# A conditioned residual on one core: loads moved to ScalarE's queue in 1 MB pieces, zeros and placing shared out anew

## The reference

```python
# x: (64, 64, 512) f32, itok: (64,) int32, weights: (200, 64, 64) f32
w = weights[itok]
out = x + jnp.einsum('bct,bcd->bdt', x, w)
```

## Time and profile before

| | |
|---|---|
| median of 3 runs | 47.75 us (47.55 to 47.91) |
| the profiled execution's own time | 47.52 us |
| its span | 45.6 us |
| PE, VectorE, ScalarE, GpSimd busy | 23.4, 14.9, 14.6, 2.6 us |
| moved by DMA | 17.83 MB: 9.44 read from HBM, 8.39 written |
| granted TensorE clock, mean | 0.981 of full |

### The profile page before, as it was taken

The page is one execution under the profiler, slowest core; times in us unless marked ns, Lnnn a source line. Parts: engine busy times, 40 slices in busy tenths (PEclk is TensorE's granted clock), DMA queues, the critical chain, the costliest instruction groups (busy, mean ns, idle before and its releaser), DMA issues.

```text
span 45.6 us, 301 instructions
## 1 busy us (share of the span) xinstructions
PE 23.4 (51%) x98; PEld 10.0 (22%) x98; DVE 14.9 (33%) x20; ACT 14.6 (32%) x18; POOL 2.6 (6%) x10
## 2 busy tenths in 40 slices
PE   0004000000000009999999789999999999930000
PEld 0004000000000004243527054534534434300000
DVE  0891000000003980009559290064064065550000
ACT  0820000000000009009999999062062063450000
POOL 4080900000000000000000000000000000000000
PEclk9999999999999999999999999999999999999975
DMA  0689999999999999999997999999998999999991
GB/s 0 108 338 431 424 417 431 417 439 424 431 431 511 431 403 417 388 460 460 460 331 280 403 424 453 381 489 446 460 417 338 431 446 403 424 439 388 417 406 47
DMA packets 2162, 17.83 MB, mean 391 GB/s; under 512 B 242, under 2 KB 242, under 8 KB 498
## 3 DMA queue, kind: packets, MB, share of 16 engines
q1 hardware_dynamic: 2016, 16.78, 89.1%
q0 software_dynamic: 144, 1.05, 5.4%
q10 hardware_dynamic: 2, 0.00, 0.0%
HBM read 9.44 MB, written 8.39 MB: 391 GB/s over the span
## 4 chain that ended last, share of the span: by engine, by line
PE 43%; DMA 21%; DVE 10%; ACT 7%; issue 5%; POOL 2%; POOLq 1%
PE product L156 31%; DMA gathered<-weights,table_row 21%; PE product L160 12%; DVE w_all L186 5%; ACT y_sb L116 4%; ACT w_diag L111 3%; POOL w_diag L128 2%; DVE w_diag L168 2%; DVE y_sb L195 2%; DVE gathered L183 1%; POOLq L36 1%; DVE piece L171 0%; DVE one L169 0%
## 5 line engine op out<-in xcount | busy, mean ns | idle before, releaser
L160 PE MATMUL product<-x_sb,w_all 64*64 64x512 f32 x64 | 8.9, 698 | 13.0 <-DVE w_all L186 12.9
L156 PE MATMUL product<-x_sb,w_diag 128*128 128x512 f32 x32 | 14.0, 594 | 0.3 <-issue 0.3
L191 DVE COPY y_sb<-product 128x1024 f32<-128x1024 f32 x7 | 8.6, 1225 | 12.6 <-PE product L156 7.2
L116 ACT COPY y_sb<-product 128x1024 f32<-128x1024 f32 x7 | 7.1, 1012 | 8.5 <-PE product L156 6.3
L111 ACT COPY w_diag<-w_all 64x256 f32<-64x256 f32 x8 | 5.1, 637 | 14.6 <-DVE w_all L186 14.4
L156 PEld LDWEIGHTS product<-x_sb,w_diag 128*128 128x128 f32 x32 | 6.0, 190 | 8.3 <-issue 8.3
L160 PEld LDWEIGHTS product<-x_sb,w_all 64*64 64x64 f32 x64 | 3.5, 207 | 17.6 <-DVE w_all L186 13.0
L183 DVE TENSOR_TENSOR gathered<-gathered,piece 128x64 f32<-128x64 f32 x1 | 0.3, 270 | 10.0 <-DMA gathered<-weights,table_row 10.0
L139 PE MATMUL product<-one,row_along 1*128 1x1 f32 x2 | 0.6, 344 | 3.6 <-DVE row_along L175 3.6
L186 DVE STREAM_TRANSPOSE w_all<-gathered 128x2048 f32<-128x2048 f32 x1 | 2.3, 2311 | 0.0
L195 DVE COPY y_sb<-product 128x512 f32<-128x512 f32 x2 | 1.4, 692 | 1.5 <-PE product L156 1.5
(11 more groups left out here) (4 smaller groups left out, 0.4 us busy)
## 6 DMA issues: line engine op xcount, KB each, us to landing
out<-y_sb SPq DMA_DIRECT2D x5, 1024.0 KB, 6.2
x_sb<-x SPq DMA_DIRECT2D x4, 1024.0 KB, 8.3
x_sb<-x SPq DMA_DIRECT2D x2, 2048.0 KB, 19.9
out<-y_sb SPq DMA_DIRECT2D x1, 2048.0 KB, 6.7
out<-y_sb SPq DMA_DIRECT2D x2, 512.0 KB, 4.3
condition<-conditions ACTq DMA_DIRECT2D x1, 0.2 KB
gathered<-weights,table_row POOLq DMA_INDIRECT x1, 9.7
```

Of the source, the lines that this page charges most:

```text
L116: nc.scalar.copy(y_sb[:, 4 * turn:4 * turn + 2, :], product[turn % SETS][0][:, :, :]).then_inc(moved_by_act, 1)
L156: product_of = nc.tensor.matmul(product[turn % SETS][j][:, g, :], w_diag[:, n - 4 * TILED, :], x_sb[:, n, :], start=True, stop=True)
L160: product_of = nc.tensor.matmul(product[turn % SETS][h][halves(g), j, :], w_all[halves(h), :, n], x_sb[halves(h), n, :], start=True, stop= ...
L191: nc.vector.tensor_copy(y_sb[:, 4 * turn + 2:4 * turn + 4, :], product[turn % SETS][1][:, :, :]).then_inc(moved_by_dve, 1)
```

## The change

- All loads are issued from ScalarE's queue, as eight loads of one turn each. The conditions' load and the stores are issued from the sync queue; stores too are of one turn each, and the last turn in two rounds as before. Every run is 8 KB (4 KB in the two last stores).
- The memsets of `w_diag` on VectorE (L168) and GpSimd (L128) go. VectorE sets a 128x1 tile `zero`, and ScalarE copies it, as a broadcast, over the off-diagonal blocks, two copies of 64x1024, after it has issued the loads.
- Placing is shared: ScalarE copies the upper half (`halves(0)`) and VectorE the lower (`halves(1)`), one copy of 64x256 each per turn in turns 0 to 3.
- The semaphores for zeroing and placing go, since the copies to `y_sb` behind them on the same engines already make TensorE wait. VectorE waits for `pieces_set` before the diagonal add; GpSimd no longer does.

```diff
-    LOADS = [(0, 0), (1, 1), (2, 2), (3, 3), (4, 5), (6, 7)]
-    STORES = [(0, 0), (1, 1), (2, 3), (4, 4), (5, 5), (6, 6)]
...
         @block.sync
         def _(sp):
-            for first, last in LOADS:
-                pairs = pairs_of(first, last)
-                sp.dma_start(x_sb[:, pairs, :], x[:, pairs, :]).then_inc(x_loaded[first], 16)
-            for first, last in STORES:
-                sp.wait_ge(moved_by_act, last + 1)
-                sp.wait_ge(moved_by_dve, last + 1)
-                pairs = pairs_of(first, last)
-                sp.dma_start(out[:, pairs, :], y_sb[:, pairs, :]).then_inc(stored, 16)
+            sp.dma_start(condition[:, :, :], conditions).then_inc(condition_loaded, 16)
+            for turn in range(LAST):
+                sp.wait_ge(moved_by_act, turn + 1)
+                sp.wait_ge(moved_by_dve, turn + 1)
+                sp.dma_start(out[:, pairs_of(turn), :], y_sb[:, pairs_of(turn), :]).then_inc(stored, 16)
...
         @block.scalar
         def _(act):
-            act.dma_start(condition[:, :, :], conditions).then_inc(condition_loaded, 16)
+            for turn in range(TURNS):
+                act.dma_start(x_sb[:, pairs_of(turn), :], x[:, pairs_of(turn), :]).then_inc(x_loaded[turn], 16)
+            act.wait_ge(zero_set, 1)
+            for h in range(PAIR):
+                nc.scalar.copy(w_diag[halves(h), :, (1 - h) * D:(2 - h) * D],
+                               zero[halves(h), :].unsqueeze(2).to_broadcast([C, PAIRS - 4 * TILED, D]))
+            act.wait_ge(w_ready, 1)
             for turn in range(TURNS):
                 if turn < TILED:
-                    later = slice(4 * turn, 4 * turn + 4)
-                    act.wait_ge(w_ready, 1)
-                    for h in range(PAIR):
-                        nc.scalar.copy(w_diag[halves(h), later, h * D:(h + 1) * D],
-                                       w_all[halves(h), :, pairs_of(TILED + turn, TILED + turn)].rearrange("p d n -> p n d")
-                                       ).then_inc(w_placed, 1)
+                    nc.scalar.copy(w_diag[halves(0), pairs_of(turn), 0:D],
+                                   w_all[halves(0), :, pairs_of(TILED + turn)].rearrange("p d n -> p n d"))
...
         @block.gpsimd
-            pool.wait_ge(pieces_set, 2 * (P // Q))
-            nc.gpsimd.memset(w_diag[halves(1), :, 0:D], 0.0).then_inc(w_zeroed, 1)
...
         @block.tensor
-                if turn in x_loaded:
-                    pe.wait_ge(x_loaded[turn], 16)
+                pe.wait_ge(x_loaded[turn], 16)
...
-                if turn == TILED:
-                    pe.wait_ge(w_zeroed, 2)
-                if turn >= TILED:
-                    pe.wait_ge(w_placed, PAIR * (turn - TILED + 1))
...
         @block.vector
-            nc.vector.memset(w_diag[halves(0), :, D:PAIR * D], 0.0).then_inc(w_zeroed, 1)
+            nc.vector.memset(zero[:, :], 0.0).then_inc(zero_set, 1)
...
+            dve.wait_ge(pieces_set, 2 * (P // Q))
...
+            dve.wait_ge(w_ready, 1)
             for turn in range(LAST):
+                if turn < TILED:
+                    nc.vector.tensor_copy(w_diag[halves(1), pairs_of(turn), D:PAIR * D],
+                                          w_all[halves(1), :, pairs_of(TILED + turn)].rearrange("p d n -> p n d"))
                 dve.wait_ge(multiplied, turn + 1)
```

More of the change, by code:

```diff
@@ L48, in conditioned_residual_kernel @@
         one = sbuf("one", [1, 1], fp32)
+        zero = sbuf("zero", [P, 1], fp32)
         piece = sbuf("piece", [P, K], fp32)
@@ L58, in conditioned_residual_kernel @@
                    for s in range(SETS)]
-        x_loaded = {first: semaphore(f"x_loaded{first}") for first, _ in LOADS}
+        x_loaded = [semaphore(f"x_loaded{turn}") for turn in range(TURNS)]
         condition_loaded = semaphore("condition_loaded")
         one_set = semaphore("one_set")
+        zero_set = semaphore("zero_set")
         rows_along = semaphore("rows_along")
@@ L69, in conditioned_residual_kernel @@
         w_ready = semaphore("w_ready")
-        w_zeroed = semaphore("w_zeroed")
-        w_placed = semaphore("w_placed")
         multiplied = semaphore("multiplied")
@@ L79, in halves, with pairs_of @@
             return slice(h * C, (h + 1) * C)
-        def pairs_of(first, last):
-            return slice(4 * first, 4 * last + 4)
+        def pairs_of(turn):
+            return slice(4 * turn, 4 * turn + 4)
         def round_of(turn, j):
@@ L100, in _ @@
                 sp.dma_start(out[:, round_of(LAST, j), :], y_sb[:, round_of(LAST, j), :]).then_inc(stored, 16)
-            sp.wait_ge(stored, 16 * (len(STORES) + 2))
+            sp.wait_ge(stored, 16 * (TURNS + 1))
         @block.scalar
         def _(act):
-            act.dma_start(condition[:, :, :], conditions).then_inc(condition_loaded, 16)
+            for turn in range(TURNS):
[5 more added lines that the diff above has]
+            act.wait_ge(w_ready, 1)
             for turn in range(TURNS):
                 if turn < TILED:
-                    later = slice(4 * turn, 4 * turn + 4)
-                    act.wait_ge(w_ready, 1)
-                    for h in range(PAIR):
-                        nc.scalar.copy(w_diag[halves(h), later, h * D:(h + 1) * D],
-                                       w_all[halves(h), :, pairs_of(TILED + turn, TILED + turn)].rearrange("p d n -> p n d")
-                                       ).then_inc(w_placed, 1)
+                    nc.scalar.copy(w_diag[halves(0), pairs_of(turn), 0:D],
+                                   w_all[halves(0), :, pairs_of(TILED + turn)].rearrange("p d n -> p n d"))
                 if turn < LAST:
```

## The result

| | before | after |
|---|---|---|
| median of six runs of each | 47.88 us | 48.39 us |
| profiled execution, its span | 47.52, 45.6 us | 48.08, 46.2 us |
| last copy to y_sb ends | 41.0 us | 40.0 us |

The ratio is 1.012, with a 95% interval of 1.008 to 1.017. I had forecast 47.2 us, and 48.39 is outside my range too.

The account below looks back on a forecast made before the run. Transfers were taken to bound the kernel: 0.27 (switch) plus 0.21 (8 KB runs) is 0.48 us, so the profiled 47.52 becomes 47.04. With medians 0.23 above the profiled run it expected 47.25, rounded to 47.2 us; range 46.6 to 48.1.

Parts of the forecast that it names:

- The transfers set the end: Whole kernel: DMA transfers bound it, so 1.7 us of earlier compute is worth nothing by itself.
- The front: Start, before the turns: without the memsets L175 ends 1.1 us sooner; gather issued at 3.5 rather than 4.61.
- The turns: Turns 0 to 4: shared placing stops TensorE waiting for ScalarE, 0.6 us gained; TensorE ends at 38.6.
- 8 KB instead of the 16 KB store: Stores in 30 to 35 us: 8 KB runs lift the rate from 408 GB/s, gaining 0.21 us.
- The switch: 23 to 26 us, loads to stores in one queue: two queues take back a net loss of 0.27 us.
- The mixture: From 20.6 us: loads and stores alternate on the engines for some 6.8 us at 426 GB/s.
- Rival 2: Mixed stretch: engines lose time turning from load to store packets, 366 GB/s, 1.1 us cost, 48.4 us; chance 0.16.
- Rival 1: The switch: loss comes from changing HBM reads to writes, not queue order; no telling change, 47.6 us; chance 0.25.

Follow-up runs that it names:

- e4: Kernel before with only the changed kernel's compute (ScalarE's zeros, shared placing), old load and store lists, old queues; ratio 1.006.
- e3: Kernel before with 8 KB runs alone: eight loads and seven stores of one turn, all on the sync queue; ratio 1.003 (0.999 to 1.008).
- g4: Changed kernel stripped to loads and stores, no computation; each turn stored from x_sb once its load has landed; 45.54 us.
- e1: Changed kernel with its queues undone: loads and stores from the sync queue, conditions from ScalarE's; 8 KB runs and new compute stay; ratio 1.013.
- c1: g4 with the first two turns copied inside SBUF (x_sb to y_sb) as each lands, stores after the seventh load; no time given.
- c2: g4 with the two early transfers going from HBM to HBM, other stores after the seventh load; no time given.
- e2: Kernel before with queues swapped alone: six loads with old lists from ScalarE's queue, conditions and stores from the sync queue; ratio 1.006.
- c3: g4 with the first and fifth turns stored as each lands, the rest after the seventh load; no time given.
- g3: Changed kernel with the first store held until the last load has landed; ratio 1.029 (1.020 to 1.039).
- g1: Changed kernel with the first store held until the load of turn 6 has landed; ratio 0.988, 47.41 us; second time 0.995, 47.44 us.
- g2: e1 with the first store held until the load of turn 6 has landed; ratio 0.996, 47.52 us.

## Why the prediction was wrong, point by point

- **The transfers set the end:** right, and shown by e4 and by the changed kernel itself, whose last copies ended 1.5 and 1.1 us sooner than before's, and which ran no faster for it. It holds only while the transfers are as slow as in the kernel before: in e3, without a dip, the queue was all but empty at the end, and the last copy at 41.5 came too late for a gain.
- **The front:** right. 1.1 us forecast, 1.16 measured, L165 at 0.28 us. That the memset on GpSimd had caused the 1.06 isn't shown by itself, since VectorE's memset went as well. The Trainium skill, "SBUF — State Buffer", section "Who interferes with whom", says that a two-port VectorE operation and a GpSimd one shut each other out for a whole instruction; the 1.06 us with a memset beside it and the 0.28 without agree.
- **The turns:** prices right (VectorE's placing 0.39 against 0.35, zero copies 1.04 each against 1.0); TensorE's end 39.25, within the 38 to 39.3 that I named. I had 38.6, as turns 0 to 3 took 9.25 us rather than 8.7.
- **8 KB instead of the 16 KB store: a misreading, and the second term that failed.** 429 against 408 GB/s in 30 to 35 would be 0.25 us where I had 0.21, but that is luck. The 442 of 26 to 30 and the 408 of 30 to 35 are one effect of how 16 KB packets are booked, and I used one half for each term. Together, before and after:

```profile
26.00:35.00 9.00, 8.68 (x21) 3.92 (x22) 3.68 (x3) 4.54 (x6) 0.00 (x0) 1.00 1.00 423
```

```profile
26.00:35.00 9.00, 9.00 (x22) 3.99 (x21) 3.03 (x3) 2.39 (x3) 0.00 (x0) 1.00 1.01 428
```

That is 0.1 us. e4 keeps the 16 KB store and has 437 in 30 to 35, and e3, with 8 KB runs alone, gains no time. All that the kernel before lacked in 13 to 35 us was 0.31 us, so 0.48 was not there to be gained.
- **The switch: this step failed.** I put the net loss of before at 0.27 us, took it for the order in the queue, and had it vanish with two queues. It grew instead, to 93 x 3 = 0.28 MB or 0.65 us in 23 to 26, with nothing given back behind (0.67 us over 13 to 35, where before lost 0.31). The error is in its cause. I read the rate of 23 to 26 as the place where loads end and stores begin. It is what the first long store does to loads still under way, before its own packets move, and how much of it falls on loads depends on how soon the store comes. All the microseconds gained in compute went into making that sooner. I had priced this gain at nothing; it had a negative price.
- **The mixture:** I had stores alternating with loads from 20.6 us, 6.8 us long. In the changed kernel it hardly exists, since the store's packets wait from 21.15 to 25, when the loads are nearly done. Where it does exist, in g4, it has the 426 GB/s that I took. The delay stood in the trace of before: the gather is issued at 4.61 and its packets share the engines in 9 to 10 us; the first of them move behind 8.5. I used these rows for the sharing and didn't carry over the delay.
- **Rival 2** gave 48.4 us, which is the measured time by luck, since its mechanism is wrong: an engine that loses time at each turn from load to store would have shown in g4 at 12 us, and doesn't. Rival 1 was right about the queues: one queue and two differ little, as the changed kernel and e1 show (1.012 and 1.013), and the two with the store held (0.988 and 0.995 in two trials of two queues, 0.996 with one). The Trainium skill, "DMA: Bandwidth & Descriptors", section "Issuing engines are not separate DMA queues", says that more issuing engines save issue time alone; these ratios agree. The other half of rival 1, a cost of turning to writes of HBM, falls by c1, which has the fall without any such write, and c2, which writes and has none.
- **Left over:** 0.12 us of the loss lies in 2.5 to 13 us, where the first packets are slow in every profile; whether the queues have a part in it isn't shown. Nor is why the swap alone (e2) costs 0.6%, with a dip smaller than before's; its profile has 416 GB/s over 13 to 35 us to before's 420, and the loss lies in 30 to 35 (395), not in the dip. And the bytes left at 44.5 explain 0.4 of the 0.56 us between the profiled executions; the rest is open.

## What to carry to other kernels

Where transfers bound a kernel, find the stretches in which the engines are busy and the bytes are few, and ask which transfer had just been issued; it may not have moved a byte yet. An engine that delivers sooner is not free there: look at what its results set off, and try to hold that back by one wait (here one `wait_ge` ahead of the first store, for the last but one load, turned 1.012 into 0.988 to 0.995). Hold it only so far that its start-up is still covered: held for one load more, the kernel ran at 1.029. And look at what sets the end once the transfers are faster, since e3 lost its dip and gained nothing.

## What the hardware showed that I had not expected

- The first long DMA that reads SBUF, issued while loads from HBM keep the 16 engines full, slows these loads to 284 to 298 GB/s over 3 us (7 to 10 us in g4, c1 and c3, issue at 5.5), 0.9 to 1.0 us of work. Its own packets come over 4 us behind the issue, and only some 0.8 us behind it in g3 (issued at 25.32), where the engines are idle. The second such DMA, 13 us later in c3, costs nothing, nor does one from HBM to HBM in c2.
- A DMA of 64 KB from SBUF (512 bytes per partition) didn't count as the first. Where between 64 KB and 1 MB the line lies, whether it is size or length of run, and what in the engines it is, stays open.
- Issued when the last load's packets have about 2 us to go (22.73 in g1, where they end by 24.75), the same first store costs nothing that shows (421 and 423 GB/s in g1 and g2).
